# Ten products of the identity with itself on TensorE, ahead of the first sums of A and its transpose

## What is computed

```python
# first half, b = 0..3; h = ctx_512[b] (512 x 128)
sim = einsum(Q, K) / (sqrt(32) * 4)                # 512 x 512
k = 153
threshold = top_k(sim, k)[0][:, -1:]
A = sigmoid(sim) * (sim >= threshold)
A = (A + swapaxes(A, -1, -2)) * 0.5
x = x + tanh(g_xattn) * ((1 - gamma) * layernorm(x) + gamma * A)
# second half
xt = layernorm(x).reshape(2048, 512)
probs = softmax(xt @ gate_w.T); weights, experts = top_k(probs, 2)
expert_out[e] = (silu(xt @ w1[e].T) * (xt @ w3[e].T)) @ w2[e].T
x = x + tanh(g_ffn) * sum over the two experts of weight * expert_out
```

## Time and profile before

| | before |
|---|---|
| time, median of 3 runs | 824.0 us (819.68 to 826.24) |
| the profiled execution | 824.68 us, span 823.0 us |
| granted TensorE clock, mean of the span | 0.918 of full speed |
| PE busy with products | 732.0 us (89%) |
| PE busy with weight loads | 589.9 us (72%) |
| DVE, ACT, POOL busy | 396.6, 286.8, 146.9 us |

### The profile page before, as it was taken

The page is one execution under the profiler, slowest core; times in us unless marked ns, Lnnn a source line. Parts: engine busy times, 40 slices in busy tenths (PEclk is TensorE's granted clock), DMA queues, the critical chain, the costliest instruction groups (busy, mean ns, idle before and its releaser), DMA issues.

```text
span 823.0 us, 10904 instructions
## 1 busy us (share of the span) xinstructions
PE 732.0 (89%) x3370; PEld 589.9 (72%) x3371; DVE 396.6 (48%) x930; ACT 286.8 (35%) x475; POOL 146.9 (18%) x199
## 2 busy tenths in 40 slices
PE   7393079556999999999999999999999999999996
PEld 3193046545888888888888888888888888888885
DVE  3988966562247232832266229222652382265222
ACT  4754647621135211711154116112531261253111
POOL 1371002782111000011001011010011110101110
PEclk9655577568999999999999999999999999999999
DMA  8842032655622721182115511821155127211111
GB/s 302 324 161 102 12 142 106 239 200 191 231 38 62 288 41 43 26 324 46 39 26 180 203 26 26 331 38 39 35 197 177 28 40 315 51 36 29 26 30 22
DMA packets 23727, 98.18 MB, mean 119 GB/s; under 512 B 2784, under 2 KB 3040, under 8 KB 19872
## 3 DMA queue, kind: packets, MB, share of 16 engines
q0 software_dynamic: 10992, 66.21, 26.0%
q1 hardware_dynamic: 12576, 31.81, 11.3%
q10 hardware_dynamic: 144, 0.00, 0.0%
HBM read 73.72 MB, written 24.30 MB: 119 GB/s over the span
## 4 chain that ended last, share of the span: by engine, by line
issue 72%; DVE 9%; POOL 6%; PE 5%; POOLq 3%; ACT 2%; DVEq 1%; DMA 1%; SPq 0%; ACTq 0%
POOL out L434 4%; POOL routed L399 2%; DVE front L852 2%; PE bank L504 2%; POOLq L255 1%; POOLq L433 1%; PE bank L466 1%; PE bank L502 1%; DVE top L950 1%; DVE ln_stats L810 1%; DVE front L947 1%; DVE rows_own L827 1%; POOL raw L442 1%; ACT front L705 1%; PE bank L456 1%
## 5 line engine op out<-in xcount | busy, mean ns | idle before, releaser
L546 PE MATMUL bank<-w_hi,xT_hi 128*128 128x512 f32 x560 | 225.5, 403 | 3.3 <-DVE xT_lo L1116 3.3
L547 PE MATMUL bank<-w_hi,xT_lo 128*128 128x512 f32 x560 | 222.3, 397 | 0.0
L548 PE MATMUL bank<-w_lo,xT_hi 128*128 128x512 f32 x560 | 221.7, 396 | 0.0
L754 ACT ACTIVATE act_g<-bank 128x512 f32<-128x512 f32 x70 | 41.8, 596 | 332.1 <-PE bank L548 327.6
L546 PEld LDWEIGHTS bank<-w_hi,xT_hi 128*128 128x128 f32 x560 | 105.8, 189 | 27.5 <-issue 3.7
L548 PEld LDWEIGHTS bank<-w_lo,xT_hi 128*128 128x128 f32 x560 | 105.6, 188 | 25.8
L547 PEld LDWEIGHTS bank<-w_hi,xT_lo 128*128 128x128 f32 x560 | 105.8, 189 | 23.5
L546 PE MATMUL bank<-w_hi,hT_hi 128*128 128x512 f32 x280 | 115.9, 414 | 0.0
L1132 DVE TENSOR_TENSOR hT_lo<-bank,hT_hi 128x512 fp32r<-128x512 f32 x70 | 48.4, 692 | 138.7 <-ACT hT_hi L758 138.7
L1010 DVE TENSOR_TENSOR w_lo<-raw,w_hi 128x1024 fp32r<-128x1024 f32 x88 | 104.3, 1221 | 19.0 <-ACT w_hi L670 10.5
L670 ACT ACTIVATE w_hi<-raw 128x1024 fp32r<-128x1024 f32 x88 | 91.4, 1061 | 59.3 <-PE bank L548 50.4
(11 more groups left out here) (190 smaller groups left out, 668.8 us busy)
## 6 DMA issues: line engine op xcount, KB each, us to landing
raw<-weights POOLq DMA_DIRECT2D x21, 2048.0 KB, 15.7
xtile<-routed SPq DMA_DIRECT2D x36, 260.5 KB
raw<-weights SPq DMA_DIRECT2D x3, 2048.0 KB, 7.9
xb<-x SPq DMA_DIRECT2D x4, 1024.0 KB, 11.3
raw<-xT SPq DMA_DIRECT2D x4, 1024.0 KB, 9.0
w_hi<-weights POOLq DMA_DIRECT2D x2, 2048.0 KB, 10.3
out<-xb SPq DMA_DIRECT2D x4, 1024.0 KB, 4.2
routed<-pad SPq DMA_DIRECT2D x8, 260.5 KB, 2.3
```

The source lines that it names most:

```text
L546: nc.tensor.matmul(out_ap, hi, hi_w, start=start, stop=False)
L547: nc.tensor.matmul(out_ap, lo, hi_w, start=False, stop=False)
L548: return nc.tensor.matmul(out_ap, hi, lo_w, start=False, stop=stop)
L754: nc.scalar.activation(act_g[:, s, :], bank[GATE[s]][:, :], ACT.Silu).then_inc(silu_set[s], 1)
```

## The change

Behind the small product of the settled rows, PE runs ten products more. Each has the identity `ident` as both operands, 128x128 float32, and writes the first 128 columns of bank 4. They wait for nothing and signal nothing, and nothing reads what they write.

```diff
@@ -52,6 +52,7 @@
 NEWTON = 180.5
 BIG = 3.0e38
+WARM = 10
 MOST_BLOCKS = 2 * TOKENS // P + E
@@ -490,6 +491,8 @@
             pe.wait_ge(settled_set, 1)
             nc.tensor.matmul(settled_ps, ones_f[:, :], settled[:, :], start=True, stop=True).then_inc(settled_mm, 1)
+            for _ in range(WARM):
+                nc.tensor.matmul(bank[4][:, 0:P], ident[:, :], ident[:, :], start=True, stop=True)
```

## The result

| | before | changed |
|---|---|---|
| median of 19 runs each | 820.56 us | 819.31 us |
| lowest to highest | 819.42 to 826.24 | 817.76 to 820.42 |
| ratio, with 95% interval | | 0.9967 (0.9952 to 0.9983) |
| profiled execution, span | 824.68, 823.0 us | 819.61, 818.0 us |
| granted clock, mean | 0.918 | 0.922 |

The ratio is a gain of 0.17 to 0.48%, 2.7 us at its middle. The time lies inside the range of 818.0 to 825.5 us. The forecast's point, 821.7, lies above both medians: the 824.0 us from which I started was the median of three runs, and that of 19 is 820.56. Against those 820.56 us the forecast time is 1.1 us slower, and the changed kernel is 1.25 us faster.

A forecast was written before the change was run, and what follows sets the result against it. PE's unbroken stretch from 108.46 to 137.2 us was taken to set the start of the routing, and that the full phase. Gains of 2.5 us (clock rise) and 0.5 (falls) made 3.0: 824.68 to 821.7 us, range 818.0 to 825.5.

The forecast's parts named there:

- The forecast's point: Whole kernel: likeliest time 821.7 us, from a gain of 3.0 us on the profiled execution; gain of 1.5 to 4.5, chance 0.55.
- The products' cost and cover: PE ahead of the first sums: 20 records at 0.22 us, 4.4 us, wholly in idle time, ending 0.4 us before the mask.
- The overrun at 0.40 us a record: Rival, PE ahead of the sums: products end at 111.65, 3.2 us late; time 824.5, or 827.2 with the clock unmoved; chance 0.10.
- The rise: PE's first sums: clock rises 4.1 to 5.4 us after wide work begins, at 107.7 to 109.0, saving 2.5 us.
- The falls: even_scores(0) and add_transposed(2) on PE: clock falls 2.5 to 4.2 us after narrow work begins; +0.5 us gain for both together.
- more than the sum: Rival, add_transposed(2): shifted fall leaves it mostly at full clock, up to 2.5 us more, 5.5 in all, 819.0 us; chance 0.10.
- The pass to the end: From PE's sums to the end: the 3.0 us, below DVE's 4.97 us wait for PE, is all passed on.
- The base: Starting time: profiled execution of 824.68 us, checked against a median of 824.0, against which 2.3 us of gain were counted.
- within 1%: Whole kernel: measured change stays within 8.2 us, chance 0.94; faster 0.04, slower 0.02.

The follow-up runs named there:

- twenty products: Twenty identity products instead of ten ahead of the first sums, otherwise the changed kernel; 821.59 us, ratio 0.9988 to the kernel before.
- the narrow: The changed kernel's ten products with a moving operand of 8 columns instead of 128; ratio 0.9983 to the kernel before.
- early products: The changed kernel's ten products moved ahead of the wait for the settled rows, 35 us earlier; ratio 1.0004 to the kernel before.
- twenty-six products: The changed kernel with sixteen products more, ahead of the settled rows' sum; 820.76 us, ratio 0.9978 to the kernel before.
- five products: Five identity products instead of ten ahead of the first sums, otherwise the changed kernel; 823.64 us, ratio 0.9990 to the kernel before.
- the sixteen in the experts alone: The kernel before with 16 products in the wait for the experts' second tile, none ahead of the sums; 821.58 us, ratio 0.9972.
- the wide products among the narrow ones: The kernel before with six identity products inside even_scores(0), two behind each of its first three row tiles; nine of twelve runs from 821.94 to 824.35 us.
- 22 products in the experts: The changed kernel with 22 products in the first block's wait for the second tile; 817.58 us, ratio 0.9938 to the kernel before.
- 16 products in the experts: The changed kernel with 16 products in the first block's wait for the second tile; 817.28 us, ratio 0.9924 to the kernel before.
- 64 narrow products in a row: The kernel before with add_transposed(2) ahead of even_scores(0); 825.54 us, ratio 1.0047. The same swap on the changed kernel with 16 products in the experts: 820.14 us.
- the late mask: The kernel before with 2.0 us more DVE work ahead of the settled rows' count, so mask and sums start later; 826.90 us, ratio 1.0046.

## Why the prediction was right and wrong

**The products' cost and cover: right.** 20 records in 3.92 to 4.38 us in the six profiles with ten of them close ahead of the sums, 4.4 forecast; the first transpose unmoved against the small product (4.94 us behind it, 4.95 before). The overrun at 0.40 us a record did not happen; its price was measured with twenty products.

**The rise: right in its effect, early in its time.** 2.5 us forecast, 2.63 in both profiles of the changed kernel. I had it 4.1 to 5.4 us after wide work begins; in those six profiles it came 3.0 to 4.0 us after, within the products, and with twenty products 6.0. That the wide operand does it, and that it must be close ahead, is shown by the narrow and the early products.

**The falls: the step that failed.** I took +0.5 for `even_scores(0)` and `add_transposed(2)` together, because I let the fall come 2.5 to 4.2 us after the narrow products begin, as before. (By its own terms the upper end of that working is wrong too: with a rise 4.1 us after the wide work begins at 122.6 and a fall at 123.1, 3.6 us are left low, which gains 0.7 against the 5.0 of before, not 1.0.) It came in that way in one profile of the changed kernel (12.03 us, gain 0) and not at all in the other (8.71 us, gain 3.33). The term has no size of its own. It is two cases 3.3 us apart on PE, and the sum to the first indirect DMA should have been 2.6 or 5.4, not 3.0 between them. I had "more than the sum" as a rival with its 5.5 us and 819.0 us, and gave it 0.10; it is what the first profile did, and by their times most runs.

**The pass to the end: right in kind, its limit misread.** I took DVE's 4.97 us of waiting as room. ACT had only 138.41 - 137.28 = 1.1 us, but moves ahead with PE as far as its own work lets it. In the changed kernel it waits for PE at the first four copies alone; behind them its one wait is the 1.62 us for `lead`, which DVE makes. In the six profiles with a full clock at the sums and no fall (with `even_scores(0)` in its place) the first indirect DMA comes 25.53 to 25.58 us behind the first transpose, whether ten, twenty or twenty-six products ran. That is the floor of ACT with DVE's `lead`, and the -0.56 us of the table.

**The base: the other step that failed.** I made the sum against one execution and checked it against a median of three, and saw their spread of 6.5 us as noise around a centre. It was a mixture, and a longer row of runs had its median at 820.56, 3.4 us lower, so that the forecast time came out as a loss. Against the lower cluster (820.1) the changed kernel's 819.6 gains 0.5 us, against the upper one 5. The gain of 2.3 us that I forecast against 824.0 is near the measured 2.7 in size by luck: both are a mean of things that hardly any execution does; and a chance of 0.94 for "within 1%" was right only because both are far below 8.2 us.

What remains open is why the fall in `even_scores(0)` meets most executions of the kernel before and, so far, few of the changed one. The two clusters also differ ahead of the sums: the first transpose is at 108.3 to 108.6 us in the four profiles of the upper cluster and at 107.1 to 107.5 in the three of the lower one's kind (five products, the sixteen in the experts alone, and the wide products among the narrow ones). That difference is made by 14 us, in the kernel's first products. The kernel before, and then the one with five products:

```profile
9.97 4.33 PE L466 MATMUL bank<-front 128*128 128x512 f32 x8
14.14 1.02 PE L456 MATMUL bank<-front,rows_own 128*128 128x512 f32 x2
```

```profile
9.36 3.60 PE L467 MATMUL bank<-front 128*128 128x512 f32 x8
12.79 1.02 PE L457 MATMUL bank<-front,rows_own 128*128 128x512 f32 x2
```

In the four profiles of the upper cluster these eight records take 4.21 to 4.34 us, in the three others 3.60 to 3.71, and from the next product to the first transpose it is 94.2 to 94.5 us in all seven. So the 4.5 us between the clusters are two parts: about 1.2 us, there by the second group of L456, and 3.3 us at the fall. Why the two come together is not shown, and the first does not settle the second: with 3.91 us the changed kernel had no fall, with 4.89 it had one, and with 4.57 and 4.64 (22 and 16 products in the experts) it had none. The runs between 821.5 and 823 of the kernels with more products have no profile.

## What to carry to other kernels

Where TensorE goes idle ahead of a dense stretch on the critical path, wide products that nothing reads are free if they fit the wait: enough for the clock to rise before the work begins (3.9 to 4.4 us of them here, in each of six profiles; 2.5 were too few), close ahead of the work, and not past its start. Look for every such wait, and only for those whose end sets the end: the same trick brought 2.6 us at the sums, 2.5 us at the second tile and nothing at the first. And plot the single runs of the kernel before, with their clocks, before trusting a median of three.

## What the runs showed that I had not expected

**The clock fell during narrow products, with PE busy.** PE was busy all the time in `even_scores`, with 8 columns moving a product. The clock fell 2.4 to 2.6 us after `even_scores(0)` began in five profiles and not within its 3.6 us in nine; with 64 narrow products in a row it fell 3.2 and 5.5 us after they began. By the Trainium skill, "TensorE: Matmul & The Clock Gate", Part 1, the gate follows how busy PE is; here a PE busy with weight loads and 8 columns did not raise the clock (the ten narrow products, and the 23 us of L482 at 0.50) and did not always hold it.

**Some of POOL's indirect DMAs take twice as long while DVE splits the weights.** The changed kernel, DVE and then POOL in order of time:

```profile
158.59 8.04 DVE L1025 TENSOR_TENSOR w_lo<-raw,w_hi 128x1024 fp32r<-128x1024 f32 x7
```

```profile
157.43 0.97 POOL L400 DMA_INDIRECT routed<-front,place_i  x1 [0.31 <-issue]
158.71 1.95 POOL L400 DMA_INDIRECT routed<-front,place_i  x1 [0.30 <-issue]
160.96 1.96 POOL L400 DMA_INDIRECT routed<-front,place_i  x1 [0.30 <-issue]
163.23 1.97 POOL L400 DMA_INDIRECT routed<-front,place_i  x1 [0.30 <-issue]
165.50 1.97 POOL L400 DMA_INDIRECT routed<-front,place_i  x1 [0.30 <-issue]
167.78 0.97 POOL L400 DMA_INDIRECT routed<-front,place_i  x1 [0.30 <-issue]
```

Most issues take 0.97 us. Those of 1.97 all lie beside DVE's split of the weights (128x1024), but not every issue beside it is slow: with DVE splitting from 175.57 to 180.25, the one at 178.00 took 1.96 and the two at 175.45 and 176.72 took 0.97. In the kernel before four of the 32 were slow, in the changed one five, with the late mask six. It goes with the time from the first indirect DMA to the second tile's transposes: 55.45 us before, 56.13 in the changed kernel, 56.59 with the late mask. In the other profiles it is 54.8 to 55.8 us with four slow ones and 56.1 to 56.8 with five; the 22 products in the experts, with four, have 56.68, where PE itself came late. What the two share was not tried.
